# One load of eight index words for each four of w0 rows, in place of two loads of four, with the range given at the load

## What is computed

```python
w = weights0[cond0]                               # 200 matrices of 128 x 128, index by batch
x = x + einsum('bct,bcd->bdt', x, w)
w = weights1[cond1]; bias = bias1[cond1]          # 8 matrices of 128 x 128, index by batch
x = x + einsum('bct,bcd->bdt', x, w) + bias[:, :, None]
```

## Time and profile before

| | |
|---|---|
| median of 3 runs | 347.63 us (347.43 to 348.22) |
| the profiled execution's own time | 348.84 us |
| span of its instructions | 347.1 us |
| PE busy | 266.8 us (77%) |
| DVE, ACT, POOL busy | 126.3, 96.9, 65.3 us |
| data moved by DMA | 140.80 MB, mean 406 GB/s |
| mean granted TensorE clock | 0.961 |

### The profile page before, as it was taken

The page is one execution under the profiler, slowest core; times in us unless marked ns, Lnnn a source line. Parts: engine busy times, 40 slices in busy tenths (PEclk is TensorE's granted clock), DMA queues, the critical chain, the costliest instruction groups (busy, mean ns, idle before and its releaser), DMA issues.

```text
span 347.1 us, 5157 instructions
## 1 busy us (share of the span) xinstructions
PE 266.8 (77%) x774; PEld 129.5 (37%) x774; DVE 126.3 (36%) x202; ACT 96.9 (28%) x135; POOL 65.3 (19%) x249
## 2 busy tenths in 40 slices
PE   1799991986798896979877779777679877778980
PEld 1344450442344442434433334433334433333430
DVE  3254541333334242433433344333334333334440
ACT  1133350221333133332232232422242222323230
POOL 2400222112221112221122212122221212221000
PEclk9999997899989898998999999999999999999996
DMA  7999969999999999999999999999999999999994
GB/s 306 410 409 393 378 248 351 424 418 397 417 431 415 433 423 427 417 416 427 432 425 427 427 423 432 421 436 423 419 431 425 432 430 426 423 421 440 419 405 171
DMA packets 24058, 140.80 MB, mean 406 GB/s; under 512 B 2673, under 2 KB 14322, under 8 KB 15474
## 3 DMA queue, kind: packets, MB, share of 16 engines
q1 hardware_dynamic: 23760, 140.20, 97.9%
q10 hardware_dynamic: 290, 0.53, 0.4%
HBM read 76.03 MB, written 67.11 MB: 412 GB/s over the span
## 4 chain that ended last, share of the span: by engine, by line
DMA 56%; SPq 27%; issue 9%; PE 5%; ACT 0%
DMA out<-xy 47%; SPq L127 10%; DMA xy<-x 9%; SPq L122 7%; PE y_ps L306 5%; SPq L128 4%; SPq L142 3%; SPq L145 2%; ACT xy L402 0%; PE m_ps L287 0%; SPq L159 0%; SPq L148 0%; SPq L153 0%; SPq L163 0%; SPq L154 0%
## 5 line engine op out<-in xcount | busy, mean ns | idle before, releaser
L306 PE MATMUL y_ps<-xy,m_sb 128*128 128x512 f32 x512 | 245.5, 616 | 61.3 <-DMA xy<-x 60.3
L306 PEld LDWEIGHTS y_ps<-xy,m_sb 128*128 128x128 f32 x512 | 92.9, 196 | 164.9 <-issue 164.9
L402 ACT ACTIVATE xy<-y_ps,j_pick 128x512 f32<-128x512 f32 x128 | 87.9, 687 | 233.1 <-PE y_ps L306 233.1
L378 DVE TENSOR_SCALAR xy<-y_ps,j_pick 128x512 f32<-128x512 f32 x128 | 96.1, 751 | 156.5 <-PE y_ps L306 156.5
L238 POOL COPY w_pick<-w_home 128x128 f32 x112 | 32.8, 293 | 245.4 <-issue 245.4
L287 PEld LDWEIGHTS m_ps<-j_pick,w_pick 128*128 128x128 f32 x224 | 35.4, 199 | 28.7 <-issue 28.7
L370 DVE TENSOR_TENSOR m_sb<-m_ps,j_pick 128x256 f32<-128x256 f32 x64 | 27.1, 424 | 45.2 <-PE m_ps L287 44.6
L287 PE MATMUL m_ps<-j_pick,w_pick 128*128 128x128 f32 x224 | 35.1, 281 | 0.0
L240 POOL COPY j_pick<-j_all 128x129 f32 x112 | 33.0, 295 | 0.1
L402 ACT ACT_TABLE_LOAD x7 | 9.0, 1283 | 7.9 <-POOL j_pick L252 7.8
L287 PE MATMUL m_ps<-j_pick,w_home 128*128 128x128 f32 x32 | 5.5, 297 | 6.7 <-DMA w_home<-w_t 6.7
(11 more groups left out here) (16 smaller groups left out, 2.8 us busy)
## 6 DMA issues: line engine op xcount, KB each, us to landing
xy<-x SPq DMA_DIRECT2D x30, 2048.0 KB, 15.1
out<-xy SPq DMA_DIRECT2D x29, 2048.0 KB, 13.4
w_home<-w_t SPq DMA_DIRECT2D x128, 64.0 KB
out<-xy SPq DMA_DIRECT2D x5, 1024.0 KB, 6.8
xy<-x SPq DMA_DIRECT2D x3, 1024.0 KB, 7.8
xy<-x SPq DMA_DIRECT2D x4, 256.0 KB, 12.6
j_all<-w_bias SPq DMA_DIRECT2D x1, 516.0 KB, 3.7
out<-xy SPq DMA_DIRECT2D x2, 256.0 KB, 5.1
```

The source lines that it names most:

```text
L306: nc.tensor.matmul(y_ps[:, b % YB, h, :], m_sb[:, s, k, :], xy[:, s, k, half(h)], start=True, stop=True).then_inc(y_ready, 1)
L378: nc.vector.tensor_scalar(xy[:, s, k, half(0)], y_ps[:, b % YB, 0, :], j_pick[:, s, k, D:D + 1], None, ALU.add).then_inc(left_out[b % YB], 1)
L402: nc.scalar.activation(xy[:, s, k, half(1)], y_ps[:, b % YB, 1, :], ACT.Identity, bias=j_pick[:, s, k, D:D + 1]).then_inc(right_out[b % YB ...
```

## The change

`load_w0_of` reads the words of a whole four (4 batches, 8 words) with one TENSOR_LOAD, where it read two times 4 words. `load_w0_first` reads 4 words at once, where it read two times 2. The range of the words is stated at the load (`min_val`, `max_val`), and `s_assert_within` on the index and on the word of need is gone. The waits for `w0_loaded` of both slots of a four now stand ahead of the one load of words. Which transfers are issued, and in what order, stays the same.

```diff
             def words_of(words):
                 return nc.values_load_multi_w_load_instructions(
-                    words, engines=(mybir.EngineType.SP,),
-                    skip_runtime_bounds_check_because="each word is checked against its own range below")[1]
+                    words, engines=(mybir.EngineType.SP,), min_val=0, max_val=N0 - 1,
+                    skip_runtime_bounds_check_because="the reference indexes a table of N0 rows with each cond word, "
+                                                      "and each word of need is 0 or 1")[1]
...
-                             w0_t[bass.ds(nc.s_assert_within(i, 0, N0 - 1), 1), :, :].rearrange("n k c -> (n k) c"),
+                             w0_t[bass.ds(i, 1), :, :].rearrange("n k c -> (n k) c"),
...
-            def load_w0(r, s):
-
-                sp.wait_ge(w0_loaded[s], r * (PAIR * 16))
+            def load_w0(r, s, pairs=1):
+
+                for n in range(s, s + pairs):
+                    sp.wait_ge(w0_loaded[n], r * (PAIR * 16))
                 b = r * ROUND_B + s * PAIR
-                words = words_of(load_words[0:1, bass.ds(b, PAIR), :].rearrange("o b f -> o (b f)"))
-                for k in range(PAIR):
-                    load_one(b + k, s, words[2 * k], nc.s_assert_within(words[2 * k + 1], 0, 1))
+                words = words_of(load_words[0:1, bass.ds(b, pairs * PAIR), :].rearrange("o b f -> o (b f)"))
+                for k in range(pairs * PAIR):
+                    load_one(b + k, s + k // PAIR, words[2 * k], words[2 * k + 1])
...
             def load_w0_of(r, q):
-                for s in range(q * QUAD, (q + 1) * QUAD):
-                    load_w0(r, s)
+                load_w0(r, q * QUAD, QUAD)
```

More of the change, by code:

```diff
@@ L122, in words_of, with load_w0_first @@
                 return nc.values_load_multi_w_load_instructions(
-                    words, engines=(mybir.EngineType.SP,),
-                    skip_runtime_bounds_check_because="each word is checked against its own range below")[1]
+                    words, engines=(mybir.EngineType.SP,), min_val=0, max_val=N0 - 1,
+                    skip_runtime_bounds_check_because="the reference indexes a table of N0 rows with each cond word, "
+                                                      "and each word of need is 0 or 1")[1]
             def load_one(b, s, i, needed):
                 sp.dma_start(w0_home[:, bass.ds(b, 1), :].rearrange("k b c -> k (b c)"),
-                             w0_t[bass.ds(nc.s_assert_within(i, 0, N0 - 1), 1), :, :].rearrange("n k c -> (n k) c"),
+                             w0_t[bass.ds(i, 1), :, :].rearrange("n k c -> (n k) c"),
                              cond=needed).then_inc(w0_loaded[s], 16)
-            def load_w0_first(s):
-                words = words_of(cond_words[0:1, 0, s * PAIR:(s + 1) * PAIR])
-                for k in range(PAIR):
-                    load_one(s * PAIR + k, s, words[k], None)
-            def load_w0(r, s):
-                sp.wait_ge(w0_loaded[s], r * (PAIR * 16))
+            def load_w0_first(q):
+                words = words_of(cond_words[0:1, 0, q * QB:(q + 1) * QB])
+                for k in range(QB):
+                    load_one(q * QB + k, q * QUAD + k // PAIR, words[k], None)
+            def load_w0(r, s, pairs=1):
+                for n in range(s, s + pairs):
+                    sp.wait_ge(w0_loaded[n], r * (PAIR * 16))
                 b = r * ROUND_B + s * PAIR
-                words = words_of(load_words[0:1, bass.ds(b, PAIR), :].rearrange("o b f -> o (b f)"))
-                for k in range(PAIR):
-                    load_one(b + k, s, words[2 * k], nc.s_assert_within(words[2 * k + 1], 0, 1))
+                words = words_of(load_words[0:1, bass.ds(b, pairs * PAIR), :].rearrange("o b f -> o (b f)"))
+                for k in range(pairs * PAIR):
+                    load_one(b + k, s + k // PAIR, words[2 * k], words[2 * k + 1])
             def load_quad(r, q):
@@ L179, in _ @@
             for q in range(QUADS):
-                for s in range(q * QUAD, (q + 1) * QUAD):
-                    load_w0_first(s)
+                load_w0_first(q)
                 if q < QUADS - 1:
```

## The result

| | median | range | executions |
|---|---|---|---|
| before | 347.84 us | 347.43 to 348.22 | 4 |
| after | 344.32 us | 343.54 to 344.83 | 4 |

The ratio is 0.9899, 95% interval 0.9879 to 0.992: the change takes 3.5 us off (2.8 to 4.2). The profiled execution of after took 344.28 us, with a span of 342.5 us. The granted clock of TensorE does not explain the difference: the four executions of after ran at a mean of 0.923 to 0.970, and the two at 0.923 took 343.54 and 344.83, the two at 0.965 and 0.970 took 344.28 and 344.36.

The account below looks back on a forecast made before the run. Transfers were taken as the bound, with a 3.24 us queue hole behind a slow SP. Checks 2.6 plus loads 0.67 save SP 3.3 us; leaving 0.2 of the hole gains 3.0: 347.63 - 3.0 = 344.6 us, range 343.4 to 346.4.

Parts of the forecast that it names:

- What bounds the kernel: Transfers set the time; the queue stands empty 3.24 us between 44 and 49 us because SP issues a store late.
- Checks, 2.6 us for eight rows: SP, load of (1, 0) to store of (0, 2): swapping checks nets 0.33 us per row, 2.6 us (2.1 to 3.1).
- REGISTER_ALU: Comparison each w0 row gains on SP, priced at 0.09 us between a floor of 0.033 and a ceiling of 0.153.
- Loads of words, 0.67 us: Ahead of the store of (0, 2): two loads of words go (0.34 + 0.45), two waits cost 0.12; net 0.67 us.
- I take no growth: The two remaining loads, now of eight words, keep their 0.59 and 0.53 us; growth to 1.60 would cost 2.1 us.
- The sum, 3.3 us (2.8 to 3.9): SP's saving from checks (2.6) and loads of words (0.67), of 13.67 us up to the store of (0, 2).
- The load of (1, 0) "does not move": This load of x stays at 34 us despite earlier SP work, since it waits for two round 0 stores.
- One for one, until the hole is gone: Queue idle time at 44 to 49 us shrinks by SP's saving, up to 3.24 us; 0.2 left, gain 3.0 us.
- B (long loads): Rival: each load of eight words takes 1.6 us, SP saves 1.2, the hole keeps 2 us; 346.4 us, chance 0.08.
- A: The forecast: the hole at 44 to 49 us closes wholly or to half a microsecond; 343.4 to 345.2 us, chance 0.75.
- C: Rival, no change: the issuer is early but the time does not move; 347.6 us within 0.5, chance 0.10.
- D: Rival, slower: earlier stores make reads and writes disturb each other, the loop's rate falls 2%; 349.7 us, chance 0.05.

Follow-up runs that it names:

- before, second profile: The unchanged kernel before, profiled again to see whether the empty stretch at 44 to 48 us recurs; 347.92 us in one execution.
- round 0 only: Kernel before with only the rows of round 0 (`load_w0_first`) in the new form: joined words, range at load, no checks; 348.08 us against 347.75, ratio 0.9991.
- ahead of loop only: Kernel before with only the two `load_w0_of` calls between round 0 and the loop, (1, 0) and (1, 1), in the new form; 348.36 us, ratio 1.0007.
- in loop only: Kernel before with only the `load_w0_of` call inside the loop in the new form; 347.82 us, ratio 0.9981.
- joined loads only: Kernel before with one load of words per four and all checks kept; 348.18 us against 347.71, ratio 1.0004.
- checks only: Kernel before with the range given at the load and checks removed, words still loaded in pairs; 345.16 us against 347.71, ratio 0.9925.
- the change again: The whole change unaltered, timed again beside the kernel before in a later group; 344.45 us against 347.58, ratio 0.9901.
- all but round 0: The change without its edit to `load_w0_first`, so round 0 is as in the kernel before; 345.21 us against 347.58, ratio 0.9933.
- order, whole: Kernel before with store and load of x ahead of `load_w0_of`, in the loop and the three steps behind it; 346.56 us against 347.58, ratio 0.9969.
- change and order: The whole change plus store and load of x ahead of the w0 rows, in and behind the loop; 344.48 us against 347.58, ratio 0.9902.
- order in the loop: Kernel before with store and load of x ahead of `load_w0_of` in the loop only, steps behind it in old order; 349.14 us, ratio 1.0025.
- more checks: Kernel before with two further checks of the index of each w0 row; 358.20 us against 347.71, ratio 1.0292.

## Why the prediction was right

The step on which all rested holds for the change: SP's checks kept a store waiting while the transfer queue stood empty, and with the checks gone the hole and its 3.5 us went together. Another way to close the hole, the order of the issues, gained less, for a reason of its own (below). Point by point:

*What bounds the kernel.* Less work on SP closed the hole and the time fell; more work opened a second hole and the time rose. Another order closed it too and gained 1.1 us.

*SP's time, taken apart.* Added up from the same profiles, between the issue of the load of (1, 0) and that of the store of (0, 2), in us: SP's loads of words, its issues of ten transfers, and the rest (checks, addresses and the gaps between instructions).

| kernel | SP time | loads of words | issues | the rest |
|---|---|---|---|---|
| before | 13.67 | 1.73 | 3.25 | 8.69 |
| before, second profile | 13.57 | 1.62 | 3.25 | 8.70 |
| round 0 only | 12.76 | 1.20 | 3.25 | 8.31 |
| ahead of loop only | 12.00 | 1.46 | 3.94 | 6.60 |
| in loop only | 13.12 | 2.49 | 3.64 | 6.99 |
| joined loads only | 13.64 | 1.38 | 3.69 | 8.57 |
| checks only | 10.38 | 1.91 | 3.46 | 5.01 |
| the change | 9.82 | 1.23 | 3.69 | 4.90 |
| the change again | 10.08 | 1.06 | 4.11 | 4.91 |

In the rest of before, in both profiles, stands one pause of 0.38 us between a check and the next calculation, which the chain that ended last shows:

```profile
46.00 0.38 issue
```

The kernels with joined loads only and in the loop only have it in their rest too. In the changed kernel it comes at 54.48, behind the store.

*Checks, 2.6 us for eight rows.* Too low. Without the pause the rest falls from 8.31 to 5.01 with the checks gone: 3.3 us, 0.41 per row in place of 0.33. The term that was mis-sized most is the REGISTER_ALU, taken at 0.09; it is 0.037, near the lower bound given. That is 0.05 of the 0.08; the gaps account for the remainder, as far as the rows tell.

*Loads of words, 0.67 us.* Nearly right where the sum was made: 0.6. In the change the loads shrink by 1.73 - 1.23 = 0.50, and the rest by a further 0.11. By source line in that stretch (count, ns min/median/max), before:

```profile
L122 SPq TENSOR_LOAD <-load_words x4: 299/416/594, 34.6 to 44.1; - x4
L127 SPq DMA_DIRECT2D w_home<-w_t x8: 124/346/356, 36.0 to 47.0; - x8
```

The change:

```profile
L123 SPq TENSOR_LOAD <-load_words x2: 521/613/705, 34.1 to 38.3; - x2
L129 SPq DMA_DIRECT2D w_home<-w_t x8: 124/354/571, 35.0 to 42.7; - x8
```

Joined loads only:

```profile
L129 SPq DMA_DIRECT2D w_home<-w_t x8: 124/346/792, 35.4 to 46.1; - x8
```

With joined loads only a like saving, 0.35 to 0.46 us by the two profiles of before, is eaten by one row of w0 whose issue took 0.79 us in place of 0.35. "I take no growth" held at these two places (0.521 and 0.705 against 0.594 and 0.530) and fails over the whole run, where a load of eight takes 1.06 to 1.34 us in the median of a kernel and two loads of four 2 x 0.686 = 1.37.

The Trainium skill ("Runtime: NRT & Kernel Launch", section "Instruction fetch mechanics") says 200 ns per register even in bulk; an estimate from it is 1.6 us for eight. The runs show 1.06 to 1.34 in the median and 0.52 for the shortest, so its figure is too high here. What follows from it, that joining wins nothing, they bear out roughly: 1.06 us for one load of eight with joined loads only, against 1.37 for two of four before, and no difference in the time.

*The sum, 3.3 us (2.8 to 3.9).* Measured 3.85 in the profile of after (13.67 - 9.82), 3.5 in the repeated run (13.57 - 10.08). The 3.85 are 3.3 of checks, 0.6 of loads and addresses and 0.4 of the pause, less 0.4 by which issues grew. The last two are in no term of the prediction and cancel in that profile; in the repeated run the issues grew by 0.86. That the total stayed within its bounds is in part luck, and the kernels with half of the change each were needed to tell the terms.

*The load of (1, 0) "does not move".* It was issued at 33.65 in place of 34.16. But with the loop only and with the new order, whose instructions up to there are those of before, it was issued at 33.62 and 33.82. The 0.5 us are the spread between executions. The stores of slots 0 to 2 went out from 22.75 on and not all at once at 27, as said. Checks fell by 128, as said. The waits at L145 rose to 108 us, not 130: 43.5 us over 25 fours is 1.7 us each and not 2.6, since loads of eight in the loop are long.

*One for one, until the hole is gone.* Right for the whole, not for the parts. What accounts for the parts is the rate over the first 100 us, since behind it all kernels of the table but the last two move 425 or 426 GB/s until 325 us. A difference of d GB/s over 100 us is d x 100 / 425 us of time. Set against the 383 of the second profile of before (a minus is faster; in the three kernels with another order only four rows of w0 stand in the SP time):

| kernel | store at | SP time | GB/s, 0 to 100 us | worth | its span against 346.1 | ratio, in us |
|---|---|---|---|---|---|---|
| joined loads only | 47.25 | 13.64 | 383 | 0 | +0.3 | +0.1 |
| ahead of loop only | 47.27 | 12.00 | 384 | -0.2 | +0.7 | +0.2 |
| in loop only | 46.74 | 13.12 | 384 | -0.2 | 0.0 | -0.7 |
| round 0 only | 46.40 | 12.76 | 389 | -1.4 | -0.9 | -0.3 |
| all but round 0 | 44.63 | 10.94 | 393 | -2.4 | -2.5 | -2.3 |
| checks only | 44.14 | 10.38 | 396 | -3.1 | -2.9 | -2.6 |
| the change again | 44.03 | 10.08 | 396 | -3.1 | -3.1 | -3.4 |
| the change | 43.47 | 9.82 | 399 | -3.8 | -3.6 | -3.5 |
| order, whole | 40.98 | 7.16 | 399 | -3.8 | -2.0 | -1.1 |
| change and order | 39.35 | 5.66 | 404 | -4.9 | -3.6 | -3.4 |
| order in the loop | 40.97 | 7.16 | 399 | +2.0 | +0.9 | +0.9 |
| more checks | 55.26 | 15.50 | 352 | +8.9 | +10.4 | +10.2 |

The last two also lose in the loop, at 414 and 422 GB/s: -3.8 + 11 x 225 / 425 = +2.0 us, and 31 x 100 / 425 + 3 x 225 / 425 = 7.3 + 1.6 = +8.9 us. For the order in the loop that is more than its hole of 2.9 us; its rate stays low, at 324 to 377 GB/s, until 310 us. With the exception of the other orders this account meets the spans within 1.5 us, and the whole change within 0.2. It says where the time went and not why, since with equal rates behind 100 us little else can differ.

Why did one part alone move the store so little? The table of SP's time tells. Ahead of the loop and in the loop, the new form took 1.7 us each off the rest (the pause left out), together the 3.4 of the change. Ahead of the loop, 0.7 of it was lost to longer issues, one of 1.04 us, and the load of (1, 0) was 0.9 us late; in the loop, 0.8 to longer loads of words, one of 1.28 us, and 0.4 to issues. The kernel with only round 0 in the new form has unaltered instructions there and yet needs 0.8 us less than the second profile of before: its loads of words took 0.30 us each, and the pause fell elsewhere. Such is the spread from one profile to the next. In the times the three single parts have intervals of 1.2 us and more (-0.9 to +0.3, -0.4 to +0.9, -1.3 to 0.0 us), and with the rates they say that a part alone gave less than its share.

*Rivals.* B (long loads) was right for the loop, where loads of eight took 1.28 us in the median, and wrong ahead of the store, where they took 0.52 and 0.71; the time is A's. C and D fell: the time moved, and the loop's rate is 426 and 425 GB/s. The chance of 0.06 for slower is 0.01 below what D and the remainder add up to; nothing hangs on it.

*What stays open.* The two kernels with the new order throughout moved as much by 100 us as the change or more, and ended no earlier than it, one of them 1.6 us later. It is not SP's speed that sets them apart but the order. SP's timelines of the change and of the order alone, the same two loads of x, thirteen fours apart:

```profile
147.15 0.35 SPq L148 DMA_DIRECT2D xy<-x  x1
...
280.80 0.35 SPq L148 DMA_DIRECT2D xy<-x  x1
```

```profile
147.00 0.34 SPq L145 DMA_DIRECT2D xy<-x  x1
...
282.16 0.34 SPq L145 DMA_DIRECT2D xy<-x  x1
```

Between these loads lie 133.65 us in the one and 135.16 in the other. The three kernels with another order need 135.0 to 135.5 us, with a slow SP as with a fast one, and all kernels with the old order but the one with more checks 133.2 to 134.3, the kernel before among them (one profile of each). So the hole closed by order is won and about 1.4 us of it are given back in the loop. What in the order does this was not tried, and the rates, 426 GB/s in both, are too coarse to show it: 1 GB/s is 0.5 us there. The rival put on record, a ratio above 0.996 with an idle queue at 325 to 335, came as well: from 325 to 329 the order alone has shares of 0.76 and 0.68. But by then its loads were already late, and the second profile of before has such a dip too (0.76 and 0.63 from 329 to 333).

At the end, the chains of waits that ended last read, for the change and order together,

```profile
310.88 13.71 DMA xy<-x
324.60 0.23 issue
```

and for the change alone,

```profile
316.76 1.95 PE y_ps L307 x4
...
324.84 1.95 PE y_ps L307 x4
```

The one waits until 324.60 for its last large load, the other has had PE in work since 316.76 and reaches the same matmuls at the same time.

## What to carry to other kernels

- Work on the issuing engine is worth time where the transfer queue runs empty behind it, and little where the queue stays full. Find the stretch in the slices, then count what the issuer does ahead of it, down to checks of registers.
- Slack is one-sided. Taking 4 us from SP ahead of the first stores (26.85 to 22.75) brought 0.3 us by itself and 0.8 us on top of the rest, neither clear of the noise, since loads of x covered it; adding 6.4 us there (to 33.25) emptied the queue. Before adding work to an issuer that looks idle, ask how much of its cover is left in each place, not in the mean.
- To attribute a gain to the parts of a change, run the halves. A sum may be right by terms that it lacks, and moving the order of issues may open the same hole elsewhere, or slow the loop.

## What was not expected of the hardware

A load of words into SP's registers does not go by their number alone. In the first 20 us two words took 0.477 us in the median and four 0.306, and the shortest eight took 0.521; over the whole run four took 0.55 to 0.83 in the median of a kernel, eight 1.06 to 1.34. What lengthens them in the loop was not isolated.

An issue of a transfer can hold up SP. One row of w0 took 3.2 us to issue in after (the 3215 ns above, near 15 us, when SP had run ahead), against at most 0.38 in the kernel before (its second profile):

```profile
L127 SPq DMA_DIRECT2D w_home<-w_t x128: 82/342/378, 3.4 to 301.0; - x128
```

So an issuer that is made faster can give part of it back at once. Near 15 us this costs nothing, since the queue is full then. Between the load of (1, 0) and the store of (0, 2) it cost 0.44 us of SP's time in after and 0.86 in the repeated run, where one row took 0.99 us to issue. That such an issue waits because many transfers are outstanding fits, but was not isolated.

A pause of 0.35 to 0.38 us between two of SP's instructions (the 0.38 at 46.00 above) stands once between 46 and 57 us in most profiles, at different instructions. When it falls ahead of an awaited store it counts. What it is was not tried.

A full share does not mean a full rate. From 34 to 60 us the change has a share of 1.02 and moves 380 GB/s:

```profile
34.00:60.00 26.00, 21.79 (x66) 10.63 (x65) 10.32 (x16) 8.84 (x12) 6.47 (x24) 0.99 1.02 380
```

The kernel with both the change and the other order has 1.01 and 400 there:

```profile
34.00:60.00 26.00, 23.14 (x71) 11.79 (x70) 10.73 (x17) 9.53 (x13) 5.14 (x20) 0.96 1.01 400
```

The change issues sixteen rows of w0 in that stretch, the other twelve. That small rows keep the engines occupied and carry less fits this, and was not tried by itself.
